# Where the edge loop of a graph layer folds its messages, and when its sums are joined

## What is computed

```python
N, E, H, ED = 1250, 21250, 512, 64
msg = jax.nn.relu(x[src] + edge_attr @ W_e + b_e)              # E x H, x after a layer norm
aggr = jax.ops.segment_sum(msg, dst, num_segments=x.shape[0])  # N x H
h = (1.0 + eps) * x + aggr
h = jax.nn.silu(_bn(h @ W1 + b1, g1, beta1))
h = h @ W2 + b2
...
```

## Time and profile before

| what | us |
|---|---|
| median of the runs | 691.48 |
| lowest, highest | 682.82, 692.97 |
| the profiled execution, its own time | 687.2 |
| its span, first to last instruction | 685.4 |

### The profile page before, as it was taken

One profiled execution on the slowest core, in us unless ns is written; L12 is line 12 of the kernel. 1 busy time (PEld: TensorE's weight loads), 2 busy tenths in 40 slices (PEclk: granted clock), 3 DMA queues, 4 the chain that ended last, 5 costly groups with the idle time before them and its releaser, 6 DMA issues.

```text
span 685.4 us, 11467 instructions
## 1 busy us (share of the span) xinstructions
PE 565.7 (83%) x3733; PEld 357.3 (52%) x3733; DVE 370.0 (54%) x946; ACT 305.9 (45%) x612; POOL 295.7 (43%) x248
## 2 busy tenths in 40 slices
PE   2489898888979989879999994920499999999990
PEld 2333333333323333335555553710499999999990
DVE  7557565756655766656648837878613233232010
ACT  3547565656555656555558206420023333333330
POOL 3388887878888788600000000000224454453431
PEclk9989899999896999898999998755589999999996
DMA  9679878698879888606303006750048999943322
GB/s 242 168 201 209 205 193 218 190 221 198 203 201 200 211 201 213 186 9 245 123 1 123 0 1 226 229 214 0 20 136 242 251 268 257 254 117 55 57 31 27
DMA packets 75245, 108.74 MB, mean 159 GB/s; under 512 B 32120, under 2 KB 36784, under 8 KB 75208
## 3 DMA queue, kind: packets, MB, share of 16 engines
q0 software_dynamic: 43712, 53.95, 33.7%
q1 hardware_dynamic: 31392, 54.14, 26.7%
q10 hardware_dynamic: 104, 0.17, 0.1%
HBM read 95.25 MB, written 12.79 MB: 158 GB/s over the span
## 4 chain that ended last, share of the span: by engine, by line
PE 59%; POOL 14%; issue 10%; DVE 7%; DMA 4%; ACT 2%; DVEq 1%; another core or an unknown queue 0%; POOLq 0%; ACTq 0%; SPq 0%
PE bank L1249 12%; PE bank L1406 10%; PE bank L1419 10%; POOL big L451 8%; PE bank L1203 7%; POOL pair L451 6%; PE bank L1217 4%; PE bank L1219 3%; PE bank L1265 3%; DMA big<-node_rows,edge_home 2%; PE bank L1432 2%; PE bank L1387 1%; PE bank L1396 1%; PE bank L1212 1%; PE bank L1181 1%
## 5 line engine op out<-in xcount | busy, mean ns | idle before, releaser
L461 POOL DMA_INDIRECT big<-token_rows,idx x32 | 32.5, 1016 | 271.3 <-DVE idx L1110 265.8
L575 ACT ACTIVATE big<-bank 125x512 f32<-125x512 f32 x170 | 100.0, 596 | 102.3 <-DVE bank L898 55.7
L451 POOL DMA_INDIRECT big<-node_rows,edge_home x90 | 112.1, 1246 | 48.0 <-issue 47.7
L1203 PE MATMUL bank<-big,edge_home 125*64 125x256 f32 x700 | 122.5, 433 | 9.6 <-DVE aggT L877 7.6
L451 POOL DMA_INDIRECT pair<-node_rows,edge_home x80 | 98.2, 1228 | 24.4 <-issue 23.8
L898 DVE SCALAR_TENSOR_TENSOR bank<-big,bank 125x512 f32<-125x512 f32 x90 | 62.2, 699 | 42.0 <-PE bank L1219 19.0
L1203 PEld LDWEIGHTS bank<-big,edge_home 125*64 125x64 f32 x700 | 36.8, 142 | 83.7 <-issue 71.9
L1217 PE MATMUL bank<-edge_home 128*125 128x512 f16 x170 | 74.9, 441 | 4.8 <-issue 4.7
L898 DVE SCALAR_TENSOR_TENSOR bank<-pair,bank 125x512 f32<-125x512 f32 x80 | 55.4, 701 | 33.4 <-PE bank L1219 20.9
L1219 PE MATMUL bank<-edge_home 66*125 66x512 f16 x170 | 69.3, 408 | 0.0
L470 POOL DMA_INDIRECT out<-rows_z,idx x32 | 47.6, 1488 | 35.5 <-ACT rows_z L693 23.6
(11 more groups left out here) (217 smaller groups left out, 948.9 us busy)
## 6 DMA issues: line engine op xcount, KB each, us to landing
raw<-in_L_ffn_w SPq DMA_DIRECT2D x12, 1024.0 KB, 6.0
pair<-in_L_ffn_w SPq DMA_DIRECT2D x8, 1024.0 KB, 7.1
pair<-in_edge_attr SPq DMA_DIRECT2D x36, 140.0 KB
raw<-in_L_gnn_W SPq DMA_DIRECT2D x16, 256.0 KB
edge_home<-in_L_ffn_w SPq DMA_DIRECT2D x4, 1024.0 KB, 8.8
xs_home<-in_L_ffn_w SPq DMA_DIRECT2D x4, 1024.0 KB, 8.3
aggT<-in_L_ffn_w SPq DMA_DIRECT2D x4, 1024.0 KB, 8.3
xs_home<-in_x SPq DMA_DIRECT2D x5, 448.0 KB
```

The source lines that it names most:

```text
L451: pool.indirect_dma_start(row(i % RING, j), None, node_rows, bass.IndirectOffsetOnAxis(src_i[:, i, j:j + 1], 0)).then_inc(row_in[i % RING] ...
L461: pool.indirect_dma_start(xg[e % XR][:, a, :], None, token_rows, bass.IndirectOffsetOnAxis(idx[:, e, a:a + 1], 0)).then_inc(xg_in[e % XR], 16)
L575: act.activation(msg[:, b * J + j, :], bank[j][0:P, :], ACT.Relu).then_inc(msg_ready, 1)
L1203: last = pe.matmul(bank[6 + b][a * WIN:(a + 1) * WIN, 0:H // 2], onehot[b][:, j, :], msg[:, b * J + j, a * (H // 2):(a + 1) * (H // 2)], s ...
```

## The change

It rewrites the order of a step on TensorE. A step n begins with edge products 0 and 1; then come the folds 3 and 4 of the step before, which complete its sum, and the transposes for step n + 1; products 2 and 3; folds 0 and 1 of this same step, into the other bank; the turn of the sum just completed; product 4; fold 2 of this step. ScalarE copies the completed sum behind relu 0 instead of at the head of the step, and copies the edge columns behind relu 1 instead of relu 0. VectorE adds the turned sum behind row sum 3 instead of row sum 2, and splits the edges behind row sum 4. Since a sum is complete in the step after its own, one sum is left for the loop's end instead of two, with two folds instead of five; the first values of the semaphores and the index of the window's base follow (one sum of zeros is added at the beginning instead of two).

```diff
             def sum_copy(n, b):
-                act.wait_ge(folded, n * J + J)
+                act.wait_ge(folded, n * J + 2 * J)
                 act.wait_ge(sum_turned, n + 1)
...
                 to, landed = edges_landed(w, g, b, place)
-                sum_copy(n, b)
                 for j in range(J):
+                    if j == 1:
+                        sum_copy(n, 1 - b)
+                    if j == 2:
+                        act.wait_ge(edge_tr, n + 3)
+                        edge_columns(1 - b)
                     if j == 3:
...
-                    if j == 1:
-                        act.wait_ge(edge_tr, n + 3)
-                        edge_columns(1 - b)
                     act.wait_ge(row_used, CREDIT + n * J + j + 1)
...
             run_steps(act, n_pass, SB, step)
-            for b in range(2):
-                sum_copy(n_pass * SB + b, b)
+            sum_copy(n_pass * SB, 1)
...
-            dve.sem_inc(folded, J)
+            dve.sem_inc(folded, 2 * J - 2)
...
-                base = dve.value_load(base_i[0:1, bass.ds(k, 1)], min_val=0, max_val=N - 1)
+                base = dve.value_load(base_i[0:1, bass.ds(k + 1, 1)], min_val=0, max_val=N - 1)
...
-                    if j == 2:
+                    if j == 3:
                         dve.wait_ge(sum_turned, n + 2)
                         dve.wait_ge(acc_done, n + 1)
-                        accumulate(n, b).then_inc(acc_done, 1)
-                    if j == 3:
+                        accumulate(n, 1 - b).then_inc(acc_done, 1)
+                    if j == 4:
                         dve.wait_ge(edge_hi, n + 3)
...
-            for b in range(2):
-                if b == 1:
-                    W1_low(0)
-                dve.wait_ge(sum_turned, n_pass * SB + (2 + b))
-                dve.wait_ge(acc_done, n_pass * SB + (1 + b))
-                accumulate(n_pass * SB + b, b).then_inc(acc_done, 1)
-            dve.wait_ge(acc_done, n_pass * SB + 3)
-            dve.sem_inc(agg_ready, 1)
+            W1_low(0)
+            dve.wait_ge(sum_turned, n_pass * SB + 2)
+            dve.wait_ge(acc_done, n_pass * SB + 1)
+            accumulate(n_pass * SB, 1).then_inc(agg_ready, 1)
...
-            pe.matmul(bank[6][:, 0:HK * WIN], zeros[:, 0:128], zeros[:, 0:HK * WIN],
+            pe.matmul(bank[7][:, 0:HK * WIN], zeros[:, 0:128], zeros[:, 0:HK * WIN],
...
                 pe.wait_ge(edge_cp, n + 1)
-                for j in range(J):
-                    pe.wait_ge(msg_ready, n * J + j + 1)
-                    edge_product(j, b)
-                    if j == 0:
-                        pe.wait_ge(acc_done, n + 1)
-                    fold(j, 1 - b)
-                    if j == 0:
-                        edge_transposes(n + 1, 1 - b)
-                    if j == 1:
-                        turn_sum(n, b)
+                edge_product(0, b)
+                edge_product(1, b)
+                pe.wait_ge(msg_ready, n * J + J)
+                fold(3, 1 - b)
+                fold(4, 1 - b)
+                edge_transposes(n + 1, 1 - b)
+                edge_product(2, b)
+                edge_product(3, b)
+                pe.wait_ge(acc_done, n + 1)
+                pe.wait_ge(msg_ready, n * J + J + 2)
+                fold(0, b)
+                fold(1, b)
+                turn_sum(n, 1 - b)
+                edge_product(4, b)
+                pe.wait_ge(msg_ready, n * J + J + 3)
+                fold(2, b)
 
             run_steps(pe, n_pass, SB, step)
             pe.wait_ge(msg_ready, n_pass * (SB * J) + J)
-            pe.wait_ge(acc_done, n_pass * SB + 1)
-            turn_sum(n_pass * SB, 0)
-            for j in range(J):
-                fold(j, 1)
-            turn_sum(n_pass * SB + 1, 1)
+            fold(3, 1)
+            fold(4, 1)
+            turn_sum(n_pass * SB, 1)
```

## The result

| | before | changed |
|---|---|---|
| median of 20 runs, us | 686.28 | 693.81 |
| lowest, highest | 680.43, 698.10 | 688.85, 698.59 |
| profiled execution, its span | 687.2, 685.4 | 690.83, 689.0 |
| the loop: first row sum to the last step's first, in that execution | 38.44 to 293.83 | 38.30 to 300.27 |
| the last row sum; the last addition | 298.55; 305.65 | 305.12; 310.40 |

The ratio is 1.0132, interval [1.0109, 1.0155]: 7.5 us more between the medians, where I forecast 1.9 less. The two results belong together, and what follows explains both.

A forecast was written before the change was run, and what follows sets the result against it. Gathers at 7.71 us a step were taken to pace the loop, the consumer level with them. Loop unchanged, tail -1.9 us, rest nothing: 689.6 us from a median of 691.48, range 682 to 704.

The forecast's parts named there:

- What bounds the kernel before: Loop over the edges: gathers come at 7.71 us a step, the other engines keep the same pace at 7.74.
- TensorE's lead: TensorE's records running ahead by up to a step, taken to explain most of the row sum's 1.96 us behind its product.
- (1) The switches: TensorE's order in a step: ten product-fold switches become six at 0.145 us each, step 6.37 to 5.8 us.
- second case: Rival, chance 0.20: late hand-offs don't matter in the ring, the gathers alone set the loop's end, 686.1 us.
- (2) The ring's length: Chain of waits across VectorE, ScalarE and TensorE that now closes within a step: 6.85 us against 6.37 before.
- (2) How late the hand-offs are while gathers are issued: Extra on the ring's TensorE-to-VectorE hand-off: a quarter of 1.54 us, 0.35 to 0.4, making 7.2 us a step.
- ring rival: Rival, chance 0.30: the ring sets the loop's pace through late TensorE results; at 7.7 us a step, 701.2 us.
- My formula: First row sum of the last step at 84.4 + 28.7p us, p being the step at the high clock.
- (2) The loop counted as unchanged: Loop over the edges: what the switches give back, 0.8 us in a slow step, is spent on the longer ring.
- (3) The tail: After the gathers: last relu to the sum's copy falls from 3.26 to 1.35 us, saving 1.9 us.
- (4) The rest at nothing: Another zeroed bank, a base index moved by one and agg_ready raised by the addition itself: counted as no time.
- What would show it: List of trace signs, among them no TensorE step under 6.8 us and gathers still at 7.71 us a step.

The follow-up runs named there:

- e3: The kernel before with TensorE's products and folds grouped in twos, folds still of the step before: ratio to before 0.9992 [0.9951, 1.0034].
- e2: The kernel before with rows loaded by SP in plain transfers and GpSimd's gathers left out: 639.88 us in a single run.
- e1: The changed kernel with rows loaded by SP in plain transfers and GpSimd's gathers left out: 653.09 us in a single run.
- e16: The changed kernel itself, nothing altered, measured a third time on another chip against the kernel before: ratio 0.9965 [0.9939, 0.9991].

## Why the prediction was wrong, and where it was right

*What bounds the kernel before*: right in part. Row sums waited 22.9 us for gathers, and on chips 3 and 4 every kernel with full gathers waited more (26.7 to 51.4). But e3, with TensorE's step 0.54 us shorter, waited only 3.3 on chip 2 and was no faster: there row sums wait for late products even without a ring (18 of 41 such waits in e3, 13 of 45 in the kernel before). I had put most of that down to TensorE's lead.

*(1) The switches*: right. The step was to fall from 6.37 to 5.8 us. It fell from 6.26 (e2) to 5.72 (e3), with 18 us less TensorE work in the loop. The 6.37 was a step with a small gap in it. By the Trainium skill's page "TensorEngine Tiling (Array Packing)", section Key Properties, changing the tiling mode drains TensorE; e3 agrees in sign, at (6.26 - 5.72) / 4 = 0.135 us a switch. No run shows the plain gain of the second case, 686.1 us or a ratio of 0.992: grouped without any ring it is 0.9992 [0.9951, 1.0034], because the time comes off an engine whose own work didn't set the end.

*(2) The ring's length*: right. 6.85 us from eleven rows; 6.70 to 6.76 in e1, 6.78 in the good steps after. So was its order: fifth row sum 0.34 behind the addition, no step under 6.69 (I had written 6.8), gathers at their old pace.

*(2) How late the hand-offs are while gathers are issued*: this step failed. I bounded it by 0 and 1.54 us a step and took a quarter, 0.35 to 0.4, on the ground that most of the 1.96 us before was TensorE's lead. The result has 1.91 - 1.32 = 0.59 us for the turn alone, and lateness is no even surcharge: 13 of 33 steps have nearly all of it. And the ring has a second hand-off from TensorE that I didn't count, from folds 3 and 4 to the sum's copy, ahead of relu 1: the copy at 167.61 us waited 0.89 us for the folds that had begun at 164.93, and started 1.08 behind their recorded end, 0.12 where it is on time. The mechanism was the ring rival's, to which I gave 0.30.

My formula can't be called confirmed. With the mean step at the full clock after, 7.47 us, it gives 84.4 + 28.7 x 7.47 = 298.8, near the trace's 300.27. But the kernel before has the same mean of 7.47 over its steps at the full clock, and its last step begins at 293.83, 5 us before that value. The agreement is luck.

The lateness has a size that no row of the one trace could have shown. With the same code in e16 the turn costs 1.40 - 1.32 = 0.08 us more than in e1, the gathers hold the loop, and the ratio is 0.9965; the forecast was 689.6 / 691.48 = 0.997. I had taken one profiled execution for the machine. A quarter lay between two kinds of group and described neither, and that 0.9965 is near my 0.997 is no merit of the forecast.

*(2) The loop counted as unchanged*: wrong by 6.4 us in the result's profile. I reasoned that the 0.8 us that switches give back in a slow step pays for the longer ring. The slow steps got longer instead: in each kernel 14 of the 33 steps touch the low level, and they take 8.57 us on average after and 8.10 before, while the other 19 take 7.47 in both. 14 x 0.47 = 6.6 us is the whole of the loop's loss. (With the few steps that barely touch it, 0.9 granted or more, put to the fast ones, these differ by 0.15 us and the slow by 0.36.) A low piece and a late hand-off come together, as in the step at 165.32, and a ring of 6.8 us with gathers every 7.7 has only 0.9 us a step to recover with.

*(3) The tail*: right. Last relu to the sum's copy 1.26 us (1.35 forecast), to the last addition 3.88 against 5.77: 1.9 us. So the profiled execution is 6.6 us behind at the last row sum, 4.7 at the last addition, and 3.6 at its end; where the last 1.1 us goes I didn't trace. The medians differ by 7.5 us.

*(4) The rest at nothing*: nothing speaks against it.

*What would show it*: the sign that the last row sum would come less than 7 us behind the last gather's issue watched the wrong side. It came 19.7 us behind. The sign that told was one I hadn't named: row sums no longer wait for gathers.

## What to carry to other kernels

Before an edit shortens a chain that has slack of a whole step, write down the ring that it closes within one, and keep copies and additions out of it: on one chip they cost 14 us, 2% of the kernel, and putting them one tile later gave a kernel 0.8% faster than before. Where two processes of nearly the same pace run side by side, look at which of them the joining instruction waits for: the share of its idle time by releaser tells who holds the loop, and an edit on the other side brings nothing until that changes. A result of some 1% measured on one chip may hold for that chip alone; the changed kernel is 1.3% slower in two groups of runs and 0.35% faster in a third.
